# A three-pass graph kernel on one core: GpSimd checks for room in its ring of 21 groups once for seven groups instead of once for each

## The reference

```python
def gcn_conv(x, src, dst, ew, W, b):
    deg = segment_sum(ew, dst); dinv = where(deg > 0, rsqrt(deg), 0)
    norm = dinv[src] * ew * dinv[dst]
    return segment_sum((x @ W)[src] * norm[:, None], dst) + b
...
h = relu(gcn_conv(x, src, dst, ew, W1, b1)); h = sigmoid(gcn_conv(h, src, dst, ew, W2, b2))
x = layernorm(x + h)
...
z = x @ fc_w.T; rh = edge_attr @ fc_r_w.T
e = leaky(z[src] @ aw[0] + z[dst] @ aw[1] + rh @ aw[2])
alpha = segment_softmax(e, dst)
agg = segment_sum(alpha[:, None] * (z[src] + rh), dst)
x = layernorm(x + relu(agg + z @ loop_w))
```

## Time and profile before

| | us |
|---|---|
| median of 3 runs (lowest, highest) | 4012.1 (4003.41, 4015.61) |
| the profiled execution, its own time | 4005.03 |
| its span | 4003.2 |
| granted TensorE clock, mean of the span | 0.623 of full speed |

### The profile page before, as it was taken

The page is one execution under the profiler, slowest core; times in us unless marked ns, Lnnn a source line. Parts: engine busy times, 40 slices in busy tenths (PEclk is TensorE's granted clock), DMA queues, the critical chain, the costliest instruction groups (busy, mean ns, idle before and its releaser), DMA issues. The chain is left out here.

```text
span 4003.2 us, 32754 instructions
## 1 busy us (share of the span) xinstructions
PE 1829.6 (46%) x10392; PEld 1691.8 (42%) x10392; DVE 1598.5 (40%) x7455; ACT 169.3 (4%) x292; POOL 2262.0 (57%) x2357
## 2 busy tenths in 40 slices
PE   1335553444336411244444344500466666666687
PEld 1234452343335411243343344500366556566677
DVE  3555433444446400134454457811333333222354
ACT  0001000000000000000000000100000000000010
POOL 7433666666662377566666664176455556555510
PEclk9855655556556655566555657655666666666687
DMA  4112222344444221111112211022333333333331
GB/s 107 29 29 78 72 76 74 108 118 116 113 114 128 73 53 51 39 52 52 51 52 53 52 50 39 19 54 49 87 86 87 86 78 87 85 87 86 80 93 37
DMA packets 325074, 288.01 MB, mean 72 GB/s; under 512 B 43190, under 2 KB 284781, under 8 KB 324878
## 3 DMA queue, kind: packets, MB, share of 16 engines
q0 software_dynamic: 75072, 155.50, 15.8%
q1 hardware_dynamic: 236898, 123.92, 10.8%
q10 hardware_dynamic: 12924, 6.41, 0.6%
HBM read 272.66 MB, written 13.40 MB: 71 GB/s over the span
## 5 line engine op out<-in xcount | busy, mean ns | idle before, releaser
L521 PE MATMUL ps<-SR,ring 128*128 128x128 f32 (+16 forms) x5844 | 1317.4, 366 | 1355.1 <-issue 633.2
L392 POOL DMA_INDIRECT ring<-x_d,srcC x1404 | 1353.6, 964 | 995.5 <-issue 404.3
L521 PEld LDWEIGHTS ps<-SR,ring 128*128 128x128 f32 x5844 | 1184.8, 283 | 1412.3 <-issue 1394.0
L392 POOL DMA_INDIRECT ring<-h_d,srcC x782 | 753.5, 964 | 476.1 <-issue 228.8
L524 PE MATMUL ps<-SR 128*128 128x128 f32 (+12 forms) x1948 | 512.6, 348 | 129.3 <-issue 128.1
L956 DVE TENSOR_SCALAR SR<-iota,rankC,ewC 128x128 f32<-128x128 f32 x1404 | 391.0, 353 | 415.9 <-remote 248.1
L524 PEld LDWEIGHTS ps<-SR 128*128 128x128 f32 x1948 | 429.2, 268 | 141.0 <-issue 140.9
L1057 DVE SCALAR_TENSOR_TENSOR U<-iota,rankC,U 128x128 f32<-128x128 f32 x782 | 238.1, 348 | 211.1 <-issue 210.4
L1114 DVE TENSOR_TENSOR_SCAN U<-U,ps 32x384 f32<-32x384 f32 (+2 forms) x26 | 24.5, 942 | 670.5 <-remote 613.3
L980 DVE SCALAR_TENSOR_TENSOR SR<-SR,v2B 128x128 f32<-128x128 f32 x782 | 181.9, 286 | 87.8 <-issue 87.5
L392 POOL DMA_INDIRECT ring<-in_x_dram,srcC x160 | 153.0, 957 | 96.8 <-issue 48.1
(11 more groups left out here) (182 smaller groups left out, 1017.8 us busy)
## 6 DMA issues: line engine op xcount, KB each, us to landing
SR<-in_edge_attr_dram SPq DMA_DIRECT2D x194, 512.0 KB
ring<-x_d,srcC POOLq DMA_INDIRECT x1404
ring<-h_d,srcC POOLq DMA_INDIRECT x782
U<-lo_d SPq DMA_DIRECT2D x20, 256.0 KB
x_d<-rows SPq DMA_DIRECT2D x12, 264.0 KB
x_d<-rows SPq DMA_DIRECT2D x7, 448.0 KB, 5.2
rows<-in_x_dram SPq DMA_DIRECT2D x6, 512.0 KB
h_d<-rows ACTq DMA_DIRECT2D x12, 256.0 KB
```

Source lines behind the costliest of these rows:

```text
L392: pool.indirect_dma_start(ring[:, gg % R, k, 0:width], None, (x if p == 0 and q < R0 else table)[:, :], bass.IndirectOffsetOnAxis(ap=srcC[ ...
L521: last = nc.tensor.matmul(ps[(p * NK + k) % 2][:, lo:hi], ring[:, gg % R, j, 0:D], S[:, gg % NS, j, w0:w0 + hi - lo], start=False, stop=t ...
```

## The change

GpSimd asks for room only when gg is a multiple of 7, and then for room for the next seven groups at once: it waits until `summed` stands at gg + 7 - 21 = gg - 14. As 98 is 14 times 7, a batch never crosses the end of a pass, and the `min` never cuts anything. For six of seven groups the wait is gone. No instruction changes its place or its engine; only waits go, and those that stay ask for more.

```diff
@@ -27,6 +27,7 @@
 R = 21
+RB = 7
 R0 = 20
...
@@ -385,8 +386,8 @@
-                    if gg >= R:
-                        pool.wait_ge(s("summed"), gg - R + 1)
+                    if gg >= R and gg % RB == 0:
+                        pool.wait_ge(s("summed"), min(gg + RB, (p + 1) * G) - R)
                     for k, t in enumerate(tiles(q)):
```

## The result

The changed kernel takes 4567.1 us (median of 4 runs, 4561.0 to 4574.6) against 4012.3 us (4003.4 to 4015.6) of the kernel before on the same chip: a ratio of 1.14, 95% interval 1.137 to 1.143. Forecast were 4590 us, 4070 to 4800, and slower with 0.87.

A forecast was written before the change was run, and what follows sets the result against it. No engine was taken as the bound: waits fill the time, and GpSimd's pauses set the pace. 170 + 149 + 259 = 578 us on 4005.0 gave 4583, plus 7 for the median: 4590 us, range 4070 to 4800.

The forecast's parts named there:

- The pauses are the pace-maker: GpSimd's waits for ring room: each gives TensorE and VectorE some 15 quick us.
- late starts: TensorE and VectorE instructions starting late during unbroken gathers: 25 summing matmuls in 70 us at pass 1's start.
- The price of a check: GpSimd's stop after each 56 gathers: 9 + 17 = 26 us in passes 0 and 1, 44 us in pass 2.
- The 9 us of drag behind a stop: Drag, the slowing of TensorE and VectorE by unbroken gathers, lasts 0.13 x 70 = 9 us after GpSimd stops.
- Groups summed in a run of 70 us: Groups summed during 56 gathers and the drag: 3.9 in passes 0 and 1, 2.5 in pass 2.
- The first check of each pass: Pass 0 goes on near 382 us; pass 1 waits 30 us, 24 of it drag; pass 2 starts 46 us later.
- The terms: Time added in passes 0, 1 and 2: 170, 149 and 259 us, together 578 us.
- The rule on interference: Skill's rule that DMA never contends with a compute engine; by it gathers couldn't slow TensorE and the sum would be zero.
- the unnamed pauses: GpSimd's "remote" waits, 80 without named releaser: read as the raise of `summed` reaching GpSimd only when the drag has ended.
- No change: Rival: starts are late for another reason and pauses merely coincide; time stays at 4012 us; chance 0.08.
- faster: Rival: TensorE sums seven groups in 70 + 9 us, a check costs 9 us; -215, about 3800 us; chance 0.05.
- A little slower: Rival: the drag saturates, one 9 us pause serves as well as several of 4; +79, near 4090 us; chance 0.10.

The follow-up runs named there:

- number 9: Kernel before, changed by pass: pass 0 reserve of 14 groups; pass 1 batch checks, four `iota` per third group; pass 2 one `iota` per group; 3874.4 us, 0.967.
- number 11: Kernel before plus three `iota` after each second group in pass 0, two after each group in passes 1 and 2; 3736.7 us against 4032.0, 0.929.
- number 1: Kernel before with a reserve of 14 groups instead of 20, waited for per group; 3099.5 us against 3098.35, 1.0001.
- Number 10: Kernel before with one check per 14 groups in pass 0, and GpSimd waiting for its own semaphore behind each group in passes 1 and 2; 4209.2 us, 1.050.
- numbers 4 and 2: 4: kernel before plus one `iota` after each group, 3324.9 us, 1.073. 2: changed kernel plus four `iota` after each third group, 3442.3 us, 1.111.
- numbers 10 and 12: 12: kernel before with a reserve of eight groups instead of 20, waited for per group; 3121.8 us against 3096.2, 1.007.

## Why the prediction was right

- *The pauses are the pace-maker.* Right, and shown from both sides: without the short ones the gathers of a pass take 167, 164 and 243 us longer; with artificial ones beside the long checks (number 9, pass 1) they are back at the pace of before; with more of them than before (number 11) most of the late starts are gone and the kernel is 7% quicker.
- *The price of a check.* Forecast were 26 us in passes 0 and 1 and 44 in pass 2. The ten checks behind each pass's first measure 25.5, 26.9 and 43.3 us on average.
- *The 9 us of drag behind a stop.* At the ten later checks of pass 0 TensorE starts 1 summing matmul in the first 6 us of GpSimd's stop, 10 in the next 6 and then about 4 in each us. Behind a resume it starts 35 in the first 9 us and some 0.4 in a us from 18 us on. Both lie where the prediction had them.
- *Groups summed in a run of 70 us.* Forecast 3.9 and 2.5, bounds 3.2 to 4.6 and 1.6 to 4. By counts of matmuls it was 2.3 to 5.1, on average 3.6, and 1.9 to 2.8, on average 2.5. Single cycles fall outside the bounds, the means don't. That 3.6 came at the price of 3.9 is because the rest went quicker: 26 us less 9 of drag leave 17 for 3.4 groups, 5.1 us each where 5.35 was taken.
- *The first check of each pass.* Pass 0's group 21 starts at 377.4 us (382 forecast). Pass 1's check takes 25.8 us (30), but not as 24 of drag and 6 for one more group: the last matmul of the group that it waits for ended at 1705.0, before the pause began at 1710.7, so all of it is lateness. Pass 2's takes 77.0 where the earlier trace rows had 46.0, +31, and +46 was forecast: the term that was off most.
- *The terms.* Between the last sums of the passes the time grew by 151, 162 and 243 us (1493.2, 2878.7 and 4545.7 against 1342.0, 2565.6 and 3989.8), forecast 170, 149 and 259: 556 against 578. The misses of 19, 13 and 16 us don't all go one way, so the sum looks better than its terms. Pass 0's tail shrank by 18 us rather than 7 (92.6 against the 110.6 of the earlier trace rows) and pass 1's not at all. The last gathers end at 1400.6, 2774.2 and 4386.5 us; 1410, 2790 and 4410 were named.
- *The rule on interference.* The Trainium skill's "DMA never contends with a compute engine" ("SBUF — State Buffer", "Who interferes with whom") would have made the change free. That gathers slow TensorE now has more for it than a coincidence: 25 matmuls in 70 us under unbroken gathers and 128 in 70 us under gathers with breaks, in jobs with late starts (the earlier trace rows and number 11). But 142 to 151 under unbroken gathers in a job without them (number 1) says that the rule holds there; it isn't the DMA traffic, 44 to 61 GB/s in all three, but something that some jobs have and others don't.
- *What was argued, and is borne out.* That the unnamed pauses are `summed` reaching GpSimd only when the drag is over. The pause before 2304.75 waits for `summed` to stand at 162. The last matmul of that group is the last of the 30 in the first of these two rows of TensorE, which ends at 2286.21; behind it come the late starts of the next group:

```profile
2279.72 6.49 PE L521 MATMUL ps<-SR,ring 128*128 128x4 f32 x30
2291.05 1.09 PE L521 MATMUL ps<-SR,ring 128*128 128x60 f32 x4 [4.84 <-remote]
```

The trace has a raise of `summed` at 2304.49, 18 us behind that end and 0.26 us before GpSimd goes on (275 of the 294 raises are in it, and 97 of the 99 pauses of over 1.3 us at such a wait end 0.26 us behind one). It is the common case: in 75 of the 99 (55 of 60 in passes 0 and 1) the last matmul of the awaited group had ended before the pause began, by the median 14 us before GpSimd went on in pass 0 and 20 in pass 1. So most of the "waits for room" stood before a slot that TensorE was already done with, and GpSimd hadn't been told. In the kernel before, 107 of the 294 groups have a raise of `summed` within 0.1 us of the end of their last matmul; in number 1, without late starts, all 294 do. In the changed kernel 32 of the 33 checks end 0.27 us behind the awaited matmul, so they are real waits for TensorE. Number 10 shows only that a raise which GpSimd makes itself isn't late in the first nine groups; why raises come late at all is open.
- *The rivals.* "No change" and "faster" would need the late starts to be independent of the gathers, or seven groups in 79 us; neither is seen. "A little slower" fell with number 10's pass 0.

What the prediction didn't know is that its premise depends on the job. That the changed kernel was measured where starts are late follows from no term of it: in a job of the other kind its 4590 us would have been some 1500 us off.

## What to carry to other kernels

Before a wait is taken away or merged with others, look at what the other engines do in it and in the us behind it: rows in which they suddenly follow without gaps say that the wait pays for something. Long unbroken runs of indirect DMAs on GpSimd can be such a place: a break of 2 us in each 12 bought 7% here, and one of 0.9 us in 11 only part of it. And compare such kernels in the same job alone, since breaks like these cost 7 to 11% where the late starts are absent (numbers 4 and 2; number 11's weren't run there); a version for both would have to make them only when the consumers have fallen behind.

## What the runs showed of the hardware

- The same kernel takes 4009 to 4036 us in five jobs and 3096 to 3103 us in four, and never anything between. It goes with no chip for good, by the numbers the chips are listed under: numbers 10 and 12 are listed on the same one, at 4009 and 3096 us. Whether it is the chip, its host or a state that lasts for a job stays open.
- The two kinds of job differ in their traces too. The program raises the same semaphores from the same DMAs (75,072 packets of gathers), but the traces of the late kind hold 8,880 to 14,654 such raises by DMAs and the others 42,790 to 42,847. That the late starts come with the writing of these records, and would be absent from an execution of which none are taken, is a rival that no run here tests.
- Where it is slow, instructions of TensorE and VectorE start late during unbroken indirect DMAs of GpSimd, and raises of `summed` stand in the trace long behind the matmul that makes them (18 us in the case shown above): VectorE's one-hots come 44.8 us apart deep in a run, 12 us apart with 2 us breaks. In runs of 140 us (number 10) the second half adds 0.7 to 1.6 groups to the 3.2 to 3.9 of the first. With no late starts a run of 993 us does no harm.
- What it is physically stays open. The gathers have the same length (0.94 to 0.95 us) and gap (0.30) in both kinds of job, and the granted clock differs by at most 0.13 between the stretches compared, where the matmuls differ by up to six times.
